# Filling du on TensorE in tiles of 64 rows by 32 columns in place of 64 by 64

## The chip, the cores and the metric

The kernel runs on one core of a Trainium2 chip. The metric is the device time of one execution in microseconds (us), smaller is better. The core has five engines that run side by side and meet through semaphores: TensorE (PE in the rows: matmuls; PEld: the loads of their stationary operand), VectorE (DVE), ScalarE (ACT), GpSimd (POOL) and SyncE (SP, which here only issues DMAs).

## The reference

It is one layer: a Mamba block, then a mixture of experts, each followed by a LayerNorm. The input has 4 sequences of 2048 tokens of width 256. The Mamba block, cut to what matters here:

```python
x_conv = silu(conv(x_in) + conv_b)                 # 512 channels
dt = softplus(dt_low @ dt_proj_w.T + dt_proj_b)    # 512 channels
def step(h, inp):                                  # over time; h is 512 channels x 16 states
    xt, dtt, Bt, Ct = inp
    A_bar = exp(dtt[..., None] * A)
    B_bar = (A_bar - 1.0) / safe_A * Bt[:, None, :]
    h = A_bar * h + B_bar * xt[..., None]
    y = einsum('bds,bs->bd', h, Ct) + D * xt
    return (h, y)
```

The second part routes each token to 2 of 16 experts and adds a shared expert. The change does not touch it.

## The kernel before, in words

The work is cut into 16 units of 512 tokens. A unit has 512 channels (4 chunks of 128 partitions) and 16 states, so 64 items of one chunk and one state. An item passes through three engines: ACT makes exp(dt*A) for it (line 691), DVE runs the recurrence over 512 tokens as one scan (line 1175), POOL multiplies the result with C (line 617), and PE sums the products over the states (lines 930 and 931). `h` and `hc`, which hold the items under way, have 8 slots each.

The scan's additive input is called du. The kernel writes the recurrence so that du at each step is the difference of neighbouring values of B*x, and PE makes these differences: `fill` (lines 952 to 971) multiplies 64 rows of tokens of `x_conv_rows` (the stationary operand, the channels are its columns) with a 64x128 matrix of steps, `b_steps` (the moving operand: 64 token columns for each of two states). The result goes to `g_ps`, which has two buffers of 1024 columns, one for each e. A fill serves one chunk and two states; it consists of 4 blocks of time (k), 2 halves of the rows (r) and, in the innermost loop of line 968, the halves of the 128 channels. There are 32 fills in a unit, 512 in all. Afterwards DVE adds 16 edge values in place (`join`, line 1166) and scans twice from `g_ps` (line 1175). The fill of the next use of the buffer waits for those scans (line 963).

TensorE is addressed in tiles: a matmul of 64 rows and 64 columns takes a quarter of the 128x128 array, and four such matmuls on different quarters can be under way together. The rows of the stationary operand's partitions choose the row half, the partitions of the output the column half. Quarters are used by the fill, by the sums over states (`add_quarters`, lines 926 to 931), by the convolution (line 1036) and by the dt projection (line 1055). The skip product (line 1067) has 17 rows and is placed in tiles of 32 rows by 64 columns. The others (lines 1018, 1021, 1045, 1081, and so on) use the array whole. An fp32 matmul appears in the trace as two records of MATMUL and two of LDWEIGHTS, so the 16 matmuls of a fill are 32 records of each.

The order on PE is written out by hand. For a unit, m runs over the 64 items; tables such as FILL_AT and SUM_AT (lines 334 and 336) say at which m each fill and sum stands, and PLACE (line 328) where the projections, transposes and so on stand between them. Each engine goes through its own order strictly; the counters of the semaphores, du_ready (one step for each fill), scanned, hc_ready and summed, tie them together.

After the last unit comes the second part (from line 1310 on), which does not contain fills.

Of the kernel before, what the change touches and what calls it, by code (L numbers as in the profile page):

```python
# [28 lines left out]
P = 128  # L29
# [37 lines left out]

BY_SCALAR = (2, 4, 6, 7)
HALVES = (slice(0, HALF_ROWS), slice(HALF_ROWS, P))


def count(unit, per, add):

    return per * unit + add
# [12 lines left out]
def wait(eng, sem, value):  # L87

    if value > 0:
        eng.wait_ge(sem, value)  # L90
# [59 lines left out]
def mamba(nc, d):  # L150
# [5 lines left out]
    with ExitStack() as ctx:  # L156
# [241 lines left out]
        def emptied_all(eng, u, tiles):  # L398

            most = {}  # L400
            for t in sorted(tiles, key=ORDER.get):
                most[bank_of(u, t)] = t
            for bank, t in most.items():
                eng.wait_ge(emptied[bank], tiles_before(u, t) + 1)
# [8 lines left out]
        def host(kind, c, u):  # L413

            return u if c >= 2 else u - 1
# [13 lines left out]
        def scalar_steps(j):  # L429
            return sum(k in BY_SCALAR for k in range(j))  # L430
# [479 lines left out]
        def _(pe):  # L910
# [41 lines left out]
            def fill(u, f):  # L952

                q, e = divmod(f, 2)
                j, c = q % HALF, q // HALF * 2 + e
                if q < HALF:
                    if j in BY_SCALAR:
                        pe.wait_ge(steps_by_scalar, count(u, len(BY_SCALAR), scalar_steps(j) + 1))
                    else:
                        pe.wait_ge(steps_by_vector, count(u, JS - len(BY_SCALAR), j - scalar_steps(j) + 1))  # L960
                if j == 0:
                    emptied_all(pe, host("T", c, u), [f"T{c}"])
                wait(pe, scanned, count(u, ITEMS, 4 * (q - 1) + 2 * e + 2))
                for k in range(KB):
                    for r in range(2):
                        rows = slice(HALF_ROWS * r, HALF_ROWS * (r + 1))
                        steps_of = b_steps[rows, j, k].rearrange("p t s -> p (t s)")
                        for some in HALVES:
                            one = nc.tensor.matmul(g_ps[some, e, r * T + k * P:r * T + (k + 1) * P], x_rows[rows, c, k, some],  # L969
                                                   steps_of, start=True, stop=True)  # L970
                one.then_inc(du_ready, 1)

            def tile(u, t, part):
# [72 lines left out]
                elif t in ("d1", "d3"):  # L1046
# [3 lines left out]
                    by_e = ((w_dt, dt_low), (w_dt_again[RANK:], dt_low_again[RANK:]))  # L1050
                    for half, some in enumerate(HALVES):
                        for e, (weights, rows) in enumerate(by_e):
# [6 lines left out]
                elif t in ("r1", "r3"):  # L1059
                    c = int(t[1]) - 1  # L1060
                    if c == 0:
                        pe.wait_ge(both_ready, count(u, 1, 1))
                    for half, some in enumerate(HALVES):
                        for e in range(2):
# [20 lines left out]
            for u in range(-1, UNITS):  # L1085
                if u == 0:
                    pe.wait_ge(routing_made, 7)
                    pe.wait_ge(bias_step, 7)
                    pe.wait_ge(skip_rows_ready, 2)
                for m in range(ITEMS):  # L1090
                    for su, n in due(SUM_AT, m, u):
                        add_states(su, n)
                    if u >= 0 and m in SKIP_ADD_AT:
                        add_skip(u, SKIP_ADD_AT.index(m))
                    for fu, f in due(FILL_AT, m, u):
                        if fu == 0 and f == 0:
                            pe.wait_ge(diags_ready, 2)
                        fill(fu, f)
                    for t, part in parts_at(u, m):
                        tile(u, t, part)  # L1100
                    if u == -1 and m == 7:
                        pe.wait_ge(a_inv_step, 5)
                        for c in range(CH):
                            one = nc.tensor.matmul(y_ps[0:NS, 0, c * P:(c + 1) * P], a_inv[:, c], ident[:], start=True, stop=True)
                        one.then_inc(turned_inv, 1)
# [1105 lines left out]
```

## Time and profile before

| what | value |
|---|---|
| time, median of 2 runs | 2217.26 us (2213.77 to 2220.75) |
| the profiled execution | 2220.81 us |
| its span in the trace | 2218.9 us |
| mean granted TensorE clock | 0.981 of full |
| fills begin and end | 55.5 us and 1844.4 us in the span |
| PE busy | 93% of the span |
| DVE, POOL, ACT busy | 82%, 80%, 78% |

How to read it: the span falls into the units with their fills, up to about 1844 us, and the second part, about 375 us. "Busy" for PE is the time in which at least one matmul record is open. A record lasts until its results are through, so it is longer than the time after which the next may begin; how long the array is taken by something is therefore read from the distance of starts, not from the length of a record.

### The profile page before, as it was taken

The numbers are of one execution on the slowest core, as the hardware profiler recorded it, in microseconds if no ns is written. First come the engines' busy times: TensorE is split into PE (matmuls) and PEld (weight loads), VectorE is DVE, ScalarE is ACT, GpSimd is POOL, SyncE is SP. The second block draws the span as 40 slices with busy tenths as digits, with TensorE's granted clock in tenths as the row PEclk, the third lists the DMA queues.
The fourth block names the chain that finished last, engine by engine and source line by source line (L and its number), as shares of the span: only waits on it lengthen the run. The fifth ranks groups of instructions, "written<-read, shape, count | busy, mean of one in ns | idle before, by whom it ended". The sixth has DMA issues, their size and how long they took to land. (4 is left out here: it accounts for less than half of the span.)

```text
span 2218.9 us, 68067 instructions
## 1 busy us (share of the span) xinstructions
PE 2062.6 (93%) x26118; PEld 1246.7 (56%) x26118; DVE 1825.4 (82%) x3055; ACT 1741.5 (78%) x3561; POOL 1778.1 (80%) x1699
## 2 busy tenths in 40 slices
PE   6899999999999999999999999999999796999996
PEld 2455555555555555555555555555555454788864
DVE  2898899989898989899989898988898994655556
ACT  4888888888888888898989897979898872555537
POOL 2787898979898989898989898988898994566654
PEclk9999999999999999999999999999999999999999
DMA  2232323332333232333232333232323354496668
GB/s 89 68 100 78 109 92 110 92 110 96 111 92 114 88 118 88 110 91 116 88 118 86 113 91 114 90 117 83 114 90 101 103 173 150 139 284 208 194 209 284
DMA packets 152301, 267.42 MB, mean 121 GB/s; under 512 B 26408, under 2 KB 65324, under 8 KB 151470
## 3 DMA queue, kind: packets, MB, share of 16 engines
q1 hardware_dynamic: 137198, 220.93, 33.2%
q0 software_dynamic: 14784, 42.16, 5.4%
q8 instruction: 210, 3.44, 0.6%
q14 instruction: 109, 0.89, 0.1%
HBM read 205.62 MB, written 57.39 MB: 119 GB/s over the span
## 5 line engine op out<-in xcount | busy, mean ns | idle before, releaser
L617 POOL TENSOR_TENSOR hc<-h,c_rep 128x512 f32<-128x512 f32 x1024 | 1286.4, 1278 | 212.5 <-DVE h L1175 164.9
L1175 DVE TENSOR_TENSOR_SCAN h<-g_ps,carry,h 128x512 f32<-128x512 f32 x1024 | 1274.4, 1273 | 71.7 <-ACT h L691 54.1
L691 ACT ACTIVATE h<-dt,a_mat 128x512 f32<-128x512 f32 x1024 | 695.4, 714 | 108.0 <-POOL hc L617 44.6
L969 PEld LDWEIGHTS g_ps<-b_steps,x_conv_rows 64*64 64x64 f32 x16384 | 477.1, 134 | 299.6 <-issue 209.9
L969 PE MATMUL g_ps<-b_steps,x_conv_rows 64*64 64x128 f32 x16384 | 559.0, 274 | 29.8 <-DVE h L1175 24.7
L930 PE MATMUL y_ps<-hc,dg_inv 64*64 64x512 f32 x2048 | 502.8, 605 | 14.8 <-POOL hc L617 6.5
L931 PE MATMUL y_ps<-hc,dg_inv 64*64 64x512 f32 x2048 | 501.4, 605 | 0.0
L930 PEld LDWEIGHTS y_ps<-hc,dg_inv 64*64 64x64 f32 x2048 | 139.5, 135 | 234.1 <-issue 160.4
L1662 POOL DMA_INDIRECT y_planes<-gathered,home x144 | 140.0, 972 | 106.2 <-DVE gathered L2089 81.8
L1855 PE MATMUL banks<-w_up,gathered 128*128 x576 | 148.3, 380 | 2.4 <-ACT gathered L1712 2.4
L1166 DVE TENSOR_TENSOR g_ps<-g_ps,minus_u 128x16 f32<-128x16 f32 x512 | 87.0, 170 | 76.5 <-PE g_ps L969 55.9
L1018 PE MATMUL work<-w_up 128*128 128x512 f32 x256 | 136.4, 659 | 11.5 <-DMA b_in<-in_b_in 7.4
L604 POOL DMA_INDIRECT slot_rows<-x_tok,place x116 | 122.3, 1054 | 26.1 <-issue 17.9
L1036 PE MATMUL work<-room 64*64 64x512 f32 x1024 | 122.7, 592 | 14.4 <-ACT x_conv_rows L766 12.7
L931 PEld LDWEIGHTS y_ps<-hc,dg_inv 64*64 64x64 f32 x2048 | 135.0, 135 | 0.0
L1021 PE MATMUL work<-w_up 128*128 128x512 f32 x256 | 126.0, 611 | 2.2 <-ACT gate L770 1.4
L707 ACT ACTIVATE b_steps<-steps_of,bc_tok 128x64 f32<-128x64 f32 x512 | 127.1, 340 | 0.0
L2072 DVE TENSOR_TENSOR gathered<-gathered,banks 128x128 f32<-128x128 f32 x144 | 41.1, 286 | 96.6 <-ACT gathered L1722 96.2
L1081 PE MATMUL work<-w_out,y_gated 128*128 128x256 f32 x480 | 118.4, 382 | 0.0
L1855 PEld LDWEIGHTS banks<-w_up,gathered 128*128 128x128 f32 x576 | 98.2, 190 | 10.1 <-issue 2.7
L1252 DVE SCALAR_TENSOR_TENSOR x_arg<-work,x_arg 128x512 f32<-128x512 f32 x128 | 85.3, 679 | 21.9 <-ACT work L802 21.3
L1081 PEld LDWEIGHTS work<-w_out,y_gated 128*128 128x128 f32 x480 | 85.6, 191 | 21.1 <-issue 9.8
(277 smaller groups left out, 2879.0 us busy)
## 6 DMA issues: line engine op xcount, KB each, us to landing
c_rep<-bc_rows SPq DMA_DIRECT2D x512, 256.0 KB
gathered<-slot_rows SPq DMA_DIRECT2D x144, 129.5 KB, 2.3
gathered<-y_planes SPq DMA_DIRECT2D x32, 512.0 KB, 8.4
w_up<-in_x_t SPq DMA_DIRECT2D x16, 512.0 KB, 4.8
x_raw<-in_x_tok SPq DMA_DIRECT2D x16, 512.0 KB, 4.9
out<-x_t SPq DMA_DIRECT2D x16, 512.0 KB, 3.1
x_t_rows<-y_gated SPq DMA_DIRECT2D x15, 512.0 KB, 4.3
x_t<-x_t_rows POOLq DMA_DIRECT2D x12, 512.0 KB, 5.4
```

The lines of the kernel that those rows point to most:

```text
L617: nc.gpsimd.tensor_tensor(hc[:, at_all % HCS], h[:, at_all % SLOTS], c_rep[:, at % CS], ALU.mult).then_inc(hc_ready, 1)
L691: nc.scalar.activation(h[:, (ITEMS * u + m) % SLOTS], dt[:, c], ACT.Exp, scale=a_mat[:, c, s:s + 1]).then_inc(factor_ready, 1)
L707: one = nc.scalar.activation(b_steps[:, j, k, :, s % 2], steps[:], ACT.Copy, scale=bc_tok[:, k, s:s + 1])
L930: nc.tensor.matmul(y_ps[first, 0], by[low_rows], v[low_rows], start=start, stop=stop)
L931: return nc.tensor.matmul(y_ps[second, 1], by[high_rows], v[high_rows], start=start, stop=stop)
L969: one = nc.tensor.matmul(g_ps[some, e, r * T + k * P:r * T + (k + 1) * P], x_rows[rows, c, k, some], steps_of, start=True, stop=True)
L1018: mm = nc.tensor.matmul(out, w_in[:, k, m * P:(m + 1) * P], x_t[:, of % 2, k], start=(k == 0), stop=(k == KT - 1))
L1021: mm = nc.tensor.matmul(out, w_in[:, k, m * P:(m + 1) * P], x_t[:, q, k], start=(k == 0), stop=(k == KT - 1))
L1081: mm = nc.tensor.matmul(o, y_gated[:, c, tok:tok + P], w_out[:, c], start=False, stop=(c == CH - 1))
L1175: nc.vector.tensor_tensor_scan(slot, du, slot, carry[:, batch(u), c, s:s + 1], ALU.add, ALU.mult).then_inc(scanned, 1)
L1662: nc.gpsimd.indirect_dma_start(d["y_planes"], bass.IndirectOffsetOnAxis(home[:, k % RING:k % RING + 1], 0), y_slots[:, k % BODY], None).th ...
L1855: one = nc.tensor.matmul(gu_ps[:, k % 2, 0:2 * IF], xt[:, k % 4, h * P:(h + 1) * P], w_up[:, e, h], start=(h == 0), stop=(h == KT - 1))
```

## The change

The innermost loop of `fill` goes over four groups of 32 channels instead of two groups of 64. Each matmul then has 64 rows and 32 columns; eight different tiles (two row halves times four column quarters) take part in the place of four. The moving operand is the same, the output ranges together are the same, one semaphore step still stands at the last matmul. The sums over states and the rest are as before.

```diff
+FOURTHS = tuple(slice(at, at + 32) for at in range(0, P, 32))
...
                     for r in range(2):
                         rows = slice(HALF_ROWS * r, HALF_ROWS * (r + 1))
                         steps_of = b_steps[rows, j, k].rearrange("p t s -> p (t s)")
-                        for some in HALVES:
+                        for some in FOURTHS:
                             one = nc.tensor.matmul(g_ps[some, e, r * T + k * P:r * T + (k + 1) * P], x_rows[rows, c, k, some],
                                                    steps_of, start=True, stop=True)
                 one.then_inc(du_ready, 1)
```

On PE, in the first unit, two fills around the addition of the skip term (the lines below it move down by one; a row's shape is that of the output). Before:

```order
L969 MATMUL g_ps<-b_steps,x_conv_rows 64x128 x16
L930 MATMUL y_ps<-skip,half_ident 64x512
L931 MATMUL y_ps<-skip,half_ident 64x512
L930 MATMUL y_ps<-skip,half_ident 64x512
L931 MATMUL y_ps<-skip,half_ident 64x512
L969 MATMUL g_ps<-b_steps,x_conv_rows 64x128 x16
L930 MATMUL y_ps<-hc,dg_inv 64x512
L931 MATMUL y_ps<-hc,dg_inv 64x512
```

At the same place in the changed kernel:

```order
L970 MATMUL g_ps<-b_steps,x_conv_rows 32x128 x32
L931 MATMUL y_ps<-skip,half_ident 64x512
L932 MATMUL y_ps<-skip,half_ident 64x512
L931 MATMUL y_ps<-skip,half_ident 64x512
L932 MATMUL y_ps<-skip,half_ident 64x512
L970 MATMUL g_ps<-b_steps,x_conv_rows 32x128 x32
L931 MATMUL y_ps<-hc,dg_inv 64x512
L932 MATMUL y_ps<-hc,dg_inv 64x512
```

Nothing changes its place. Each fill has 32 matmuls where it had 16, and where quarters stood beside quarters, tiles of 64 by 32 now stand beside tiles of 64 by 64. Counted over the whole order of PE: the 512 fills form 506 uninterrupted stretches; 332 of them come directly after quarters and 241 have quarters directly behind them. The number of places where the shape of the tile changes from one matmul to the next rises from 586 to 1159, by these 573.

## Rows read from the trace of the kernel before

**Rows 1.** The page: span, busy time, and slices of three engines.
```profile
span 2218.9 us, 68067 instructions
PE 2062.6 (93%) x26118; PEld 1246.7 (56%) x26118; DVE 1825.4 (82%) x3055; ACT 1741.5 (78%) x3561; POOL 1778.1 (80%) x1699
...
PE   6899999999999999999999999999999796999996
...
DVE  2898899989898989899989898988898994655556
...
POOL 2787898979898989898989898988898994566654
```

**Rows 2.** Busy time by stretch: window, length, then each engine, clock, DMA.
```profile
60.00:1844.00 1784.00, 1685.69 (x24225) 965.64 (x24221) 1601.31 (x2244) 1520.54 (x2965) 1550.85 (x1412) 0.98 0.34 103
```

**Rows 3.** Waits, 60 to 1844 us: who, for whom, us in total, times, longest.
```profile
POOL hc L617 <- DVE h L1175: 162.1, 188, 3.4
PEld g_ps L969 <- DVE h L1175: 81.9, 128, 2.8
DVE h L1175 <- ACT h L691: 53.9, 35, 2.2
DVE g_ps L1166 <- PE g_ps L969: 53.0, 96, 3.9
...
ACT h L691 <- POOL hc L617: 44.6, 58, 1.7
ACT gate L770 <- PE work L1021: 44.5, 35, 4.5
...
DVE x_raw L1203 <- PE work L1081: 20.9, 15, 1.5
```

**Rows 4.** Groups of PE by form, 60 to 1844 us: busy, mean ns, idle before.
```profile
L969 PE MATMUL g_ps<-b_steps,x_conv_rows 64*64 64x128 f32 x16303 | 556.3, 274 | 27.6 <-DVE h L1175 24.7 <-ACT x_conv_rows L766 0.7 <-issue 0.4
L930 PE MATMUL y_ps<-hc,dg_inv 64*64 64x512 f32 x2032 | 498.7, 605 | 12.7 <-DVE y_gated L1182 6.0 <-POOL hc L617 4.5
...
L1036 PE MATMUL work<-room 64*64 64x512 f32 x960 | 115.1, 592 | 12.7 <-ACT x_conv_rows L766 12.7
...
L1045 PE MATMUL work<-ident,w_up 128*128 128x128 f32 x248 | 40.4, 286 | 28.7 <-ACT dt L778 22.0 <-ACT w_up L761 2.7 <-ACT room L753 2.4
```

**Rows 5.** Timeline of PE, 1002.3 to 1012.9 us: start us, length us, what.
```profile
1002.74 1.09 PE L1067 MATMUL work<-both,skip_rows 17*64 17x512 f32 x8
1003.76 0.64 PE L930 MATMUL y_ps<-hc,dg_inv 64*64 64x512 f32 x1
...
1004.24 0.59 PE L930 MATMUL y_ps<-hc,dg_inv 64*64 64x512 f32 x1
...
1004.67 0.59 PE L930 MATMUL y_ps<-hc,dg_inv 64*64 64x512 f32 x1
...
1005.10 0.59 PE L930 MATMUL y_ps<-hc,dg_inv 64*64 64x512 f32 x1
...
1005.52 1.05 PE L969 MATMUL g_ps<-b_steps,x_conv_rows 64*64 64x128 f32 x32
1006.51 1.98 PE L1021 MATMUL work<-w_up 128*128 128x512 f32 x4
1008.42 1.10 PE L969 MATMUL g_ps<-b_steps,x_conv_rows 64*64 64x128 f32 x32
1009.35 0.59 PE L930 MATMUL y_ps<-hc,dg_inv 64*64 64x512 f32 x2
...
1011.06 1.05 PE L969 MATMUL g_ps<-b_steps,x_conv_rows 64*64 64x128 f32 x32
1011.94 1.47 PE L1036 MATMUL work<-room 64*64 64x512 f32 x12
```

**Rows 6.** Records of L969 alone at a fill's start: window, length, PE, PEld, clock.
```profile
1001.70:1001.73 0.03, 0.02 (x4) 0.03 (x4) 1.00 0.00 0
1001.73:1001.83 0.10, 0.10 (x4) 0.10 (x8) 1.00 0.00 0
```

**Rows 7.** Groups of the page: weight loads of 64 and of 128 columns.
```profile
L969 PEld LDWEIGHTS g_ps<-b_steps,x_conv_rows 64*64 64x64 f32 x16384 | 477.1, 134 | 299.6 <-issue 209.9
...
L1081 PEld LDWEIGHTS work<-w_out,y_gated 128*128 128x128 f32 x480 | 85.6, 191 | 21.1 <-issue 9.8
```

## The prediction, made before the changed kernel was run

> **What bounds the kernel now.** I read the page's slices first, then the busy time of the stretch with the fills, then the waits, and then the timeline of PE start by start. In the slices PE stands at 9 from the second to the last slice of the units, while DVE and POOL change between 8 and 9 [rows 1]. In numbers, for 60 to 1844 us: PE is busy 1685.7 of 1784.0 us (94.5%), DVE 1601.3, POOL 1550.9, ACT 1520.5 [rows 2]. So PE is the fullest engine and has 98 us of idle time in 16 units; the next has 183 us. It is not the only one that sets the pace. The waits go round: POOL waits for the scans (162 us), PE for the scans before a fill (81.9 us of the weight loads, some of it while matmuls still run), DVE for ACT (53.9 us) and for fills (53.0 us), ACT for POOL (44.6 us), and ACT and DVE for PE's other lines (44.5 us at L1021, 20.9 us at L1081) [rows 3]. PE's own idle time stands at four kinds of places above all: 28.7 us before the transposes of L1045, 27.6 us before fills, 12.7 us each before L930 and L1036 [rows 4]. A microsecond added to PE is therefore neither free nor certain to show in full.
>
> **What one fill costs.** A fill with quarters before and behind takes from 1011.06 to 1011.94, 0.88 us [rows 5]: 16 matmuls of two records on four tiles, so 8 passes of 0.11 us, in each of which four tiles stream 128 columns. A pass over 512 columns takes 0.43 us (1004.67 to 1005.10) [rows 5], four times as long, so the moving columns set the time of a pass. At a start four matmuls and four weight loads fall into 0.03 us; in the next 0.10 us no further matmul starts, only the loads of the next pass [rows 6]. The tiles wait for their streams, not for the issue.
>
> **The change, part by part.**
>
> *The matmuls themselves: 0.* 32 matmuls of two records on eight tiles are again 64/8 = 8 passes. Each streams the same 128 columns, so again 8 x 0.11 = 0.88 us. Twice the tiles do half the width; nothing is won. Four pairs start in 0.03 us, so eight need about 0.05 us of a pass of 0.11 us. The bound below zero is a stream that gets faster in a narrow tile, for which no row speaks; above, it is no overlap beyond four (both are rivals below).
>
> *Weight loads: 0.* Each has 32 columns instead of 64. 134 against 191 ns for 64 and 128 columns [rows 7] makes about 28 ns less for each. In the middle of a fill they lie under the previous pass. At a fill's first pass they are exposed, which would save at most 506 x 0.03 = 15 us; against that, the last of eight tiles starts about 0.03 us later than the last of four, at 506 exits. I let them cancel.
>
> *Changes of the tile's shape: the price.* The rows show what it costs to change the shape on PE. A fill that is followed by a matmul of another shape takes from 1005.52 to 1006.51, 0.99 us, 0.11 more than the 0.88 above. A fill that comes after another shape and has quarters behind it takes from 1008.42 to 1009.35, 0.93 us: its first pass is 0.05 us longer, because the load of the second can no longer hide. The skip product L1067 (32-row tiles) between a fill and L930 shows both: 1002.74 to 1003.76 is 1.02 us for two passes of 0.43, 0.16 more; and the first pass of L930 behind it takes 0.48 us (1003.76 to 1004.24) instead of 0.43 [rows 5]. So a change of shape costs 0.11 + 0.05 = 0.16 us on PE. The change makes 573 new ones: 332 into a fill, 241 out of one. 573 x 0.16 = 92 us. The bounds: 0 if only another row height or the whole array makes PE stop (the nearest row, L1067, changes the height and not the width), and 573 x 0.16 + 15 = 107 us with the later last tile and no gain at the loads. I take 92, because L1021 and L1067 differ from quarters in different ways and cost the same. The Trainium skill, "TensorEngine Tiling (Array Packing)", Key Properties, says that changing the tiling mode, though not changing the tile, drains TensorE, and it lists 64x64 and 64x32 as different modes. By that rule the lower bound of 0 goes away and the 92 us stand; the trace agrees as far as it shows changes (0.16 us each), but it has none of width alone between row halves.
>
> *What of the 92 us reaches the end.* All of it lies in the stretch up to 1844 us; the second part has no fill. If all of PE's 98 us of idle time [rows 2] took up the new work, nothing would show; if none did, 92 us would. The idle time is at waits for the scans, for dt, for hc and for x_conv [rows 4], and the engines behind those wait in turn for PE [rows 3]: fills that come later make later scans, so part of such a wait moves along instead of shrinking. Against that, of DVE's 183 us of idle time only 53.0 + 20.9 are ended by PE, so much of the ring runs without PE setting it. I take two fifths (39 us) as absorbed and three fifths of the idle time as staying: 92 - 39 = 53 us. What is late next is the join after each fill, then the scan, then POOL's multiplication.
>
> *Instructions.* PE gets 32768 more of them, on 68067 [rows 1]. I cost this at 0: the fetch runs beside the work, and four pairs in 0.03 us show that dispatch keeps up.
>
> The sum: 2220.8 us of the profiled execution + 53 = 2274 us. That execution lies 3.5 us above the median of the runs, so against the median it is 2217 + 53 = **2270 us**, 2.4% slower. 2% of this kernel is 44 us, about what a measurement can tell from no change.
>
> **The rivals.**
>
> *It is absorbed, or a change of width alone is cheap.* If PE stays in step when only the width changes, or the ring takes up more than half of the 92 us, the time lies between 2217 and 2261. For it: 98 us of idle time, and waits of PE for DVE at 128 loads of fills, where a stop of 0.11 us would be hidden. Against: PE at 94.5% would have to reach 97 to 99.6% of the old stretch. Chance 0.32.
>
> *The eight do not all run at once.* In the whole trace the closest sustained matmuls are the 32 records of a fill in 0.88 us, 27 ns apart. If that is a floor of issue, of the weight path or of the reading of the moving operand, which would now feed four column tiles from the same rows, 64 records take 1.76 us. That adds 0.88 x 512 = 451 us, with the 92 us 543, less at most 98 us of idle time: 2217 + 445 to 543, about 2700 us. Any smaller stretch counts too: 10 ns on each of 4096 passes are 41 us. For it: such short intervals between eight tiles are not in the trace. Against: within a pass four pairs start in 0.03 us [rows 6]. Chance 0.13, a third of it for a moderate stretch up to about 2400. The Trainium skill, "TensorE: Matmul & The Clock Gate", says in the section "Wait — 56ns, not 53.3ns?" that starts never come closer than about 25 ns. By that rule a fill would take 64 x 25 ns = 1.6 us and the kernel, by an estimate from that page, about 2217 + 0.72 x 512 + 92 - 50 = 2630 us. Here the trace disagrees inside a pass: four starts lie in 0.03 us.
>
> *Faster: a narrow tile streams faster.* If the 0.11 us of a pass belonged not to the 128 moving columns but to the 64 stationary columns (a load and its use per tile), half the width would shorten it. From 0.09 us a pass on, the shape changes are paid back (8 x 512 x 0.0225 = 92 us); at 0.055 us a fill takes 0.44 us, PE loses 225 us and gains 92, and DVE with 183 us of idle time becomes the bound: about 2217 - 80 = 2137 us. Against it: passes of 512 columns with the same 64 stationary columns take 0.43 us, four times as long [rows 5]. Chance 0.04.
>
> **How the numbers follow.** Forecast 0.51, absorbed 0.32, stretched 0.13, faster 0.04. The forecast's own range is from 2248 to 2300 (40 to 90% of 92 us). It and the absorbed case meet at 2261, the line of 2%, and a little of the forecast lies below it: faster 0.04, same 0.34, slower 0.62. For the range I leave out below the faster case and nearly complete absorption (0.10 together) and above the strong stretch (0.09): 2232 to 2350 us.
>
> **What would show it.** Right: 32768 records of the fill line with mean near 274 ns; a fill from first to last start in about 0.8 us; 1.04 us (0.88 + 0.16) from a fill's start to the matmul behind it where it stands between quarters; PE busy time up by about 90 us before the last fill; weight loads near 106 ns. Absorbed: the same rows, but PE's idle time falls by over 45 us. Cheap width: quarters follow a fill with no extra 0.11 us. Stretched: fills above 0.95 us between first record and next line, PE near 99%. My number is wrong above all if the share that reaches the end is not 0.6, which no row gives directly.

## The result and the profile after

The changed kernel takes 2286.24 us (median of 2 runs, 2283.78 to 2288.7) against 2217.26 us before: ratio 1.0307 [1.0289, 1.0325], 69 us slower. The forecast was 2270 us (+53), in a range of 2232 to 2350. The profiled execution took 2283.78 us, 63.0 more than the profiled one before.

The page of the changed kernel (compare [rows 1]; the last row is the queue that brings instructions: packets, MB, share):

```profile
span 2281.8 us, 100835 instructions
PE 2172.5 (95%) x42502; PEld 1233.5 (54%) x42502; DVE 1818.6 (80%) x3055; ACT 1744.9 (76%) x3561; POOL 1780.5 (78%) x1699
...
PE   6899999999999999999999999999999897999997
...
DVE  2898888888888879888988888988888985555557
...
q8 instruction: 338, 5.54, 1.0%
```

PE's busy time rose by 110 us; DVE, ACT and POOL do the same work in the same time. The row of the q8 queue was 210 packets before. 128 packets more for 32768 instructions more: a packet holds 256 instructions.

The busy time by stretch, from 60 us to the end of the last fill, which is now at 1907.9 us (1844.7 before, compare [rows 2]):

```profile
60.00:1907.90 1847.90, 1795.49 (x40566) 951.97 (x40562) 1595.17 (x2244) 1523.84 (x2964) 1553.61 (x1413) 0.98 0.33 101
```

This stretch is 63.2 us longer, which is the whole difference; the second part takes 374 us in both. In the stretch PE's busy time rose by 109 us (1686.4 to 1795.5) and its idle time fell from 98.3 to 52.4 us. The granted clock is 0.98 as before.

The waits in this stretch (who, for whom, us in total, times, longest; compare [rows 3]):

```profile
POOL hc L618 <- DVE h L1176: 187.5, 203, 3.7
DVE g_ps L1167 <- PE g_ps L970: 115.6, 159, 3.0
PEld g_ps L970 <- DVE h L1176: 60.8, 74, 1.6
...
ACT gate L771 <- PE work L1022: 47.1, 42, 4.8
...
DVE h L1176 <- ACT h L692: 40.0, 33, 1.5
```

DVE now waits for fills 115.6 us instead of 53.0, and PE's loads for the scans 60.8 instead of 81.9. So PE came after DVE more often than before, and POOL's wait for the scans grew with it (162 to 187.5).

The groups of PE in the same stretch (busy, mean ns, idle before with its releasers; compare [rows 4]), and after them the page's group of the fill's loads (compare [rows 7]):

```profile
L970 PE MATMUL g_ps<-b_steps,x_conv_rows 64*32 64x128 f32 x32640 | 609.5, 276 | 23.1 <-DVE h L1176 11.0 <-issue 10.3 <-ACT x_conv_rows L767 0.6
L931 PE MATMUL y_ps<-hc,dg_inv 64*64 64x512 f32 x2034 | 505.5, 613 | 1.4 <-DVE y_gated L1183 1.4
...
L1037 PE MATMUL work<-room 64*64 64x512 f32 x960 | 117.1, 601 | 11.6 <-ACT x_conv_rows L767 11.6
...
L1046 PE MATMUL work<-ident,w_up 128*128 128x128 f32 x248 | 40.3, 286 | 10.1 <-ACT dt L779 7.1 <-DVE x_arg L1253 1.3
```

```profile
L970 PEld LDWEIGHTS g_ps<-b_steps,x_conv_rows 64*32 64x32 f32 x32768 | 465.1, 106 | 375.2 <-issue 310.1
```

The idle time went down above all before the transposes (28.7 to 10.1 us), before the sums (12.7 to 1.4) and, for scans, before fills (24.7 to 11.0). What is new is 10.3 us before L970 ended by "issue": PE stood still with nothing to wait for in any other engine. The loads take 106 ns (134 before), as forecast.

The timeline around two fills (start, length, what; compare [rows 5]):

```profile
1005.15 0.64 PE L931 MATMUL y_ps<-hc,dg_inv 64*64 64x512 f32 x1
1005.16 0.64 PE L932 MATMUL y_ps<-hc,dg_inv 64*64 64x512 f32 x1
1005.19 0.64 PE L931 MATMUL y_ps<-hc,dg_inv 64*64 64x512 f32 x1
1005.21 0.64 PE L932 MATMUL y_ps<-hc,dg_inv 64*64 64x512 f32 x1
...
1008.74 1.16 PE L970 MATMUL g_ps<-b_steps,x_conv_rows 64*32 64x128 f32 x64
1009.83 0.64 PE L931 MATMUL y_ps<-hc,dg_inv 64*64 64x512 f32 x1
...
1010.31 0.59 PE L931 MATMUL y_ps<-hc,dg_inv 64*64 64x512 f32 x1
...
1010.74 0.59 PE L931 MATMUL y_ps<-hc,dg_inv 64*64 64x512 f32 x1
...
1011.70 1.33 PE L970 MATMUL g_ps<-b_steps,x_conv_rows 64*32 64x128 f32 x64
1012.97 0.28 PE L1080 MATMUL work<-b_out_parts,full 65*128 65x256 bf16 x1
```

A fill between other shapes takes 1.09 us (1008.74 to 1009.83), where 1.04 was forecast; from its first start to its last it is 0.89 us in the median (0.81 before). The first pass of quarters behind it takes 0.48 us, the second 0.43: the exposed load of 0.05 us is there. The next fill takes 1.27 us. And the four quarters at 1005.15 start over 0.06 us; in a pass where the instructions are queued they start within 0.03 us [rows 6].

A stop inside a fill, in the timeline of PE, and the packets of the instruction queue from 1058.0 to 1058.5 us:

```profile
1058.04 1.12 PE L970 MATMUL g_ps<-b_steps,x_conv_rows 64*32 64x128 f32 x61
1060.36 0.41 PE L970 MATMUL g_ps<-b_steps,x_conv_rows 64*32 64x128 f32 x3 [1.20 <-issue]
1060.69 1.10 PE L1003 MATMUL work<-w_up,w_x 128*96 128x512 f32 x2
```

```profile
q8 instruction: 1, 0.02, 11.7%
```

61 of 64 records run, then PE is idle for 1.20 us and the last three follow. 2.2 us before it goes on, the transfer of a packet of 16384 bytes of instructions begins. I call such a gap a fetch stop: over 250 ns between two starts inside one fill, no other engine that ends it, and such a packet begun 2.0 to 2.8 us ahead of the resume. There is none in the trace before, and there are 17 after (14.4 us by the distance of starts, 9.9 us of it with PE idle), which resume 2.2 to 2.7 us after their packet begins. Gaps at a fill's first record that end with a scan are not counted, though a packet precedes some of them too; they are waits for DVE.

### The profile page after: what moved, and what is told of

It is laid out like the page before. It is cut to its first block and busy times, and to the rows that moved or that the text cites. A ratio compares the mean times of both kernels' runs of the same rounds, so it can differ in the third digit from the quotient of the medians.

```text
span 2281.8 us, 100835 instructions
## 1 busy us (share of the span) xinstructions
PE 2172.5 (95%) x42502; PEld 1233.5 (54%) x42502; DVE 1818.6 (80%) x3055; ACT 1744.9 (76%) x3561; POOL 1780.5 (78%) x1699
## 5 line engine op out<-in xcount | busy, mean ns | idle before, releaser
L970 PEld LDWEIGHTS g_ps<-b_steps,x_conv_rows 64*32 64x32 f32 x32768 | 465.1, 106 | 375.2 <-issue 310.1
L970 PE MATMUL g_ps<-b_steps,x_conv_rows 64*32 64x128 f32 x32768 | 611.8, 276 | 25.2 <-DVE h L1176 11.0
L931 PE MATMUL y_ps<-hc,dg_inv 64*64 64x512 f32 x2048 | 509.0, 613 | 3.0 <-POOL hc L618 1.4
L932 PE MATMUL y_ps<-hc,dg_inv 64*64 64x512 f32 x2048 | 508.8, 613 | 0.0
L931 PEld LDWEIGHTS y_ps<-hc,dg_inv 64*64 64x64 f32 x2048 | 133.7, 135 | 246.1 <-issue 207.2
L605 POOL DMA_INDIRECT slot_rows<-x_tok,place x116 | 122.1, 1053 | 25.8 <-issue 17.6
L932 PEld LDWEIGHTS y_ps<-hc,dg_inv 64*64 64x64 f32 x2048 | 132.6, 135 | 0.2
L1856 PEld LDWEIGHTS banks<-w_up,gathered 128*128 128x128 f32 x576 | 98.2, 190 | 10.1 <-issue 2.7
L1082 PEld LDWEIGHTS work<-w_out,y_gated 128*128 128x128 f32 x480 | 85.6, 191 | 21.5 <-issue 10.1
L803 ACT ACTIVATE work<-square,shifts 128x512 f32<-128x512 f32 x128 | 85.5, 682 | 13.4 <-DVE x_arg L1253 11.4
```

The lines of the kernel that those rows point to most:

```text
L931: nc.tensor.matmul(y_ps[first, 0], by[low_rows], v[low_rows], start=start, stop=stop)
L932: return nc.tensor.matmul(y_ps[second, 1], by[high_rows], v[high_rows], start=start, stop=stop)
L1082: mm = nc.tensor.matmul(o, y_gated[:, c, tok:tok + P], w_out[:, c], start=False, stop=(c == CH - 1))
L1856: one = nc.tensor.matmul(gu_ps[:, k % 2, 0:2 * IF], xt[:, k % 4, h * P:(h + 1) * P], w_up[:, e, h], start=(h == 0), stop=(h == KT - 1))
```

## The experiments

Two causes could add up to the 69 us: the 573 new changes of shape, and 16384 more matmul records with as many loads, which must be supplied. The first four runs set the one against the other (Theory A: shape alone; the rival B: instructions alone). When each failed in its pure form, the following were judged by a mixed Theory C: about 0.06 us of the end for a new change and 4.6 ns for an additional matmul. Every ratio is against runs of the kernel before on the same chip. Each of the three groups ran on a chip of its own (before: 2216.38, 2244.41 and 2250.01 us); the second part took 374 us on the first and 395 to 404 us in the runs on the others, so only ratios are compared between groups. The last column has the mean granted clock of the kernel's runs and of those of the kernel before beside them (for the change, of the two profiled executions).

| run | shape changes | PE records | ratio to before | clock: run, before |
|---|---|---|---|---|
| before | 586 | 26118 | 1 | |
| the change | 1159 | 42502 | 1.0307 [1.0289, 1.0325] | 0.981, 0.981 |
| e1_all_narrow | 586 | 48134 | 1.0411 [1.0381, 1.0441] | 0.970, 0.981 |
| e2_sums_narrow | 1067 | 30470 | 1.0205 [1.0188, 1.0222] | 0.970, 0.981 |
| e3_short_moving | 586 | 42502 | 1.0165 [1.0148, 1.0182] | 0.972, 0.981 |
| e4_half_narrow | 1436 | 34310 | 1.0301 [1.0282, 1.0319] | 0.976, 0.981 |
| f1_row_halves | 1159 | 17926 | 1.0252 [1.0218, 1.0286] | 0.974, 0.980 |
| g_before | 449 | 26118 | 1.0291 [1.0254, 1.0329] | 0.966, 0.980 |
| g_after | 465 | 26118 | 1.0922 [1.0888, 1.0956] | 0.955, 0.980 |
| i_changed (the change) | 1159 | 42502 | 1.0420 [1.0392, 1.0449] | 0.974, 0.976 |
| i_row_halves (f1) | 1159 | 17926 | 1.0217 [1.0190, 1.0245] | 0.974, 0.976 |
| i_one_of_two | 847 | 34310 | 1.0085 [1.0057, 1.0113] | 0.974, 0.976 |
| h_skip64 | 522 | 26118 | 0.9975 [0.9955, 0.9995] | 0.975, 0.976 |

The clock is a third thing that can differ. At its lower level (1.2 GHz, 0.5 in the rows) a fill takes 1.57 us from its first start to its last in the trace before (median of four), at the upper level (2.4 GHz) 0.81. In the stretch of fills PE was at the lower level for 58 us before, 65 us with the change and 99 us in each of e1, e2 and e3. Among 94 executions, each compared with the mean of its own kernel, a granted clock lower by 0.01 went with a time longer by 13 us. By that figure the clock would be about 15 us of the loss of e1 and e2, 12 of e3 and 7 of e4 and f1 each. This is an estimate; no run holds the clock fixed, and the lower clock may itself come from what the kernel does. The change itself hardly differs from before in it.

**More instructions and no new change of shape.** The first run is the changed kernel with the sums split as well (the diff shows the first of the two sums), and the second sum, the convolution and the dt projection likewise:

```diff
-                nc.tensor.matmul(y_ps[first, 0], by[low_rows], v[low_rows], start=start, stop=stop)
+                for half in range(2):
+                    to, of = slice(first.start + 32 * half, first.start + 32 * half + 32), slice(32 * half, 32 * half + 32)
+                    nc.tensor.matmul(y_ps[to, 0], by[low_rows, of], v[low_rows], start=start, stop=stop)
...
```

> The changed kernel, with the other work that stood in quarters (sums over states, skip addition, convolution, dt projection) in tiles of 64 by 32 as well. Fills have as many matmuls as in the changed kernel, PE even more in all (24589 against 21773 and 13581 before), but the shape of the tile changes as often as before the change (586 times, not 1159). Theory A (the time went into the new changes of shape, 0.16 us each on PE, and about 0.05 us at the late end of a fill): no new change is left, the late end counts only at the 265 fills not followed by this shape; PE gets some 10 us, the time is 2217 to 2232 us. Rival B (the doubled instructions of the fills cost it, shape or not): 2286 us or more.

2304.34 us, slower than the change itself. Theory A expected nearly the time of before and failed. The waits of PE, 60 us to the last fill:

```profile
PE g_ps L975 <- issue: 44.2, 52, 3.1
PE g_ps L975 <- DVE h L1183: 12.3, 15, 3.3
```

44.2 us of PE's idle time stand before fill records without another engine to wait for; after the change alone it is 10.3 us. Fetch stops counted as above: 53, 57.5 us.

The third splits the moving columns instead of the stationary ones, so it has the instructions of the change and no new shape:

```diff
+                    for at in (0, HALF_ROWS):
+                        for r in range(2):
...
+                            for some in HALVES:
+                                to = r * T + k * P + at
+                                one = nc.tensor.matmul(g_ps[some, e, to:to + HALF_ROWS], x_rows[rows, c, k, some],
+                                                       steps_of[:, at:at + HALF_ROWS], start=True, stop=True)
```

> The kernel before, its fills in quarters, but each matmul split into two of 64 moving columns: as many matmuls in a fill (32) as in the changed kernel, no new change of shape. In the changed kernel starts come every 16.7 ns from about the 43rd record of a fill on, so with 64 records some 42 at the pace of the array (0.57 us) and 22 at 16.7 ns (0.37 us): 0.94 us in place of 0.88 for a fill. Theory A: +0.06 x 512 = 31 us on PE, 2225 to 2245 us. Rival B: as the changed kernel, 2286 us.

2254.11 us, +1.65%: above A's range and below B's figure. PE's waits in its stretch of fills:

```profile
PE g_ps L971 <- issue: 19.5, 23, 1.8
```

There are 27 fetch stops, 25.8 us. So a kernel with the change's number of instructions and no new shape loses about half of what the change loses. Not all of it is supply: four quarters with 64 moving columns follow the last four after 0.059 us, more than half of the 0.109 us for 128 columns, which adds about 37 us on PE over 512 fills (estimate), and the clock was lower (above).

**New changes of shape, few new instructions.** The second run is the kernel before with nothing changed but `add_quarters`, whose two sums are split as in the first run's diff:

> The kernel before, its fills in quarters; only the sums over states and the skip addition are in tiles of 64 by 32. 1067 changes of shape against 586 before, so 481 new ones, with 2176 more matmuls where the changed kernel has 8192 more. Theory A: 481 x 0.16 = 77 us on PE, of which about 0.6 shows: 2255 to 2280 us. Rival B (instructions): a quarter of the 69 us at most, below 2236 us.

2261.37 us, +45 us for 481 new changes: A held, B failed. There is not one fetch stop in a fill. This is the run in which shapes of the change (64 by 32 beside 64 by 64) cost time with few new instructions. Its PE is busy 1766.9 us of its stretch, 80.5 us more than before:

```profile
60.00:1885.20 1825.20, 1766.90 (x28600) 930.58 (x28603) 1604.08 (x2248) 1521.91 (x2970) 1556.38 (x1415) 0.97 0.34 101
```

The fourth puts a change inside each fill:

```diff
-                        for some in FOURTHS:
+                        for some in (FOURTHS if k < KB // 2 else HALVES):
```

> The changed kernel, but in each fill only the first two blocks of time are in tiles of 64 by 32, the last two in quarters: half of the additional matmuls (4096), but 1436 changes of shape, 850 more than before and 277 more than the changed kernel. Theory A: 850 x 0.16 = 136 us on PE, slower than the changed kernel, 2295 to 2320 us. Rival B: half of the loss, about 2252 us.

2284.06 us, between the two theories: +68 us for 850 new changes, 0.080 us each, with only 38.0 us of PE idle time left in the stretch (98.3 before).

The counterpart, with fewer instructions than before, fills in tiles of 64 rows by all 128 columns, two at once:

```diff
-                        for some in HALVES:
-                            one = nc.tensor.matmul(g_ps[some, e, r * T + k * P:r * T + (k + 1) * P], x_rows[rows, c, k, some],
-                                                   steps_of, start=True, stop=True)
+                        one = nc.tensor.matmul(g_ps[:, e, r * T + k * P:r * T + (k + 1) * P], x_rows[rows, c, k],
+                                               steps_of, start=True, stop=True)
```

> The kernel before, with the fills in tiles of 64 rows by 128 columns, two at once: 8 matmuls in a fill in place of 16 (before) or 32 (changed), the same 8 passes of 128 columns, and the same 1159 changes of shape as the changed kernel. Theory A (changes of shape alone make the loss of 69 us): about 2286 us, if anything more, as the first load has 128 columns. Theory C (both: about 0.06 us of end time for a new change of shape, about 4.6 ns for an additional matmul through the supply of instructions): 573 x 0.06 = 34 us, and some 10 us for the longer first loads: 2240 to 2268 us. Theory B (supply alone): at most 2217 us.

2297.38 us, +2.52% or 53 us, above C's figure (up to 51 us) and below A's (69). It has the same 573 new changes of shape as the change and 8192 records fewer than before, has no fetch stop, and is still slower. So something other than the supply of instructions costs over 2%. But it is not the changes of shape alone. The timeline around a fill of f1, and its stretch of fills:

```profile
1001.28 1.16 PE L968 MATMUL g_ps<-b_steps,x_conv_rows 64*128 64x128 f32 x16
1002.38 0.64 PE L930 MATMUL y_ps<-hc,dg_inv 64*64 64x512 f32 x1
```

```profile
60.00:1896.50 1836.50, 1792.42 (x16102) 992.72 (x16103) 1602.13 (x2247) 1523.90 (x2970) 1551.03 (x1414) 0.98 0.33 100
```

Its fill takes 1.10 us between other shapes, as long as the narrow one (1.09), and PE is busy 106 us more than before, against 109 with the change. Its first loads have 128 columns: the second pass starts 0.213 us after the first, where later ones follow after 0.112. So 0.10 us a fill is its own first load; the narrow fill loses 0.024 us there and 0.08 us at its last pass (below).

**Fewer changes of shape by order.** If a change costs 0.16 us of PE, moving fills next to work of another shape should pay:

In g_before the other work of every fourth item stands ahead of its fill:

```diff
+                    if m % 4 == 2:
+                        for t, part in parts_at(u, m):
+                            tile(u, t, part)
...
-                    for t, part in parts_at(u, m):
+                    for t, part in parts_at(u, m) if m % 4 != 2 else ():
```

> The kernel before, fills in quarters; where m modulo 4 is 2 the parts of the other tiles go to PE before the fill, not behind it, so that the fill stands directly ahead of the sums more often. 449 changes of shape against 586, as many matmuls. Theory C: 137 fewer changes at 0.06 us: 8 us faster, 2205 to 2212 us, unless the fills, which come later by one or two matmuls of 0.85 us, make the scans wait. Theory B: no change from the changes of shape.

In g_after it stands behind the next sums and fill:

```diff
-                    for t, part in parts_at(u, m):
-                        tile(u, t, part)
+                    for at in {2: (), 3: (m - 1, m)}.get(m % 4, (m,)):
+                        for t, part in parts_at(u, at):
+                            tile(u, t, part)
```

> The kernel before; the parts that stand where m modulo 4 is 2 go to PE one item later, behind the sums and the next fill. 465 changes of shape against 586, as many matmuls; fills come no later, projections and transposes up to 2.6 us later. Theory C: 121 x 0.06 = 7 us faster, 2205 to 2214 us, unless ACT, which takes those tiles, becomes late. Theory B: 2217 us.

Both missed: +2.9% and +9.2%. The waits of g_before and then those of g_after, each over its own stretch of fills:

```profile
DVE g_ps L1169 <- PE g_ps L969: 166.0, 111, 4.9
```

```profile
POOL hc L617 <- DVE h L1176: 381.4, 209, 7.1
...
ACT score L727 <- PE work L993: 80.9, 15, 7.1
```

In g_before each moved fill comes late and DVE waits 166.0 us for fills instead of 53.0. In g_after other products come late and ACT with them, and POOL's wait for the scans rises from 162 to 381.4 us. PE's idle time went from 98.3 to 159.6 and 257.6 us, for 137 and 121 saved changes, worth 22 and 19 us of PE. The clock fell as well: in g_after PE was at the lower level for 221 us of the stretch (58 before), and its busy time is 60 us longer with not one matmul more. In these runs the order on PE was worth more than the shapes, with the clock's part not separated.

**The disputed cost by itself.** In the next, blocks with the shape and number of a fill's matmuls run alone on PE ahead of the first unit, on data that is there (their results are not used): 40 in quarters, 40 in narrow tiles, 20 pairs in alternation, 40 in quarters with 64 moving columns.

```diff
+            def alone_narrow():
+                for k in range(KB):
+                    for r in range(2):
+                        rows = slice(HALF_ROWS * r, HALF_ROWS * (r + 1))
+                        for quarter in range(4):
+                            some = slice(32 * quarter, 32 * quarter + 32)
+                            nc.tensor.matmul(y_ps[some, r, k * P:(k + 1) * P], w_in[rows, 0, some], w_in[rows, 1, k * P:(k + 1) * P], start=True, stop=True)
...
+            for _ in range(40):
+                alone_narrow()
```

> The kernel before, and ahead of its first unit 160 blocks of matmuls on PE alone whose results are not used: 40 in the form of a fill in quarters, 40 in tiles of 64 by 32, 20 pairs of one and the other in turn, and 40 in quarters with 64 moving columns. No waits between them. 128 columns on four tiles: 0.874 us each in every theory. Theory A: narrow blocks also 0.874, a pair 2 x 0.874 + 2 x 0.16 = 2.07 us. Theory C: narrow blocks and short ones are held at 16.7 ns for each pair of load and matmul, 1.07 us a block, with stops of up to 2 us where instructions have to be fetched; a pair about 2.1 us, as the stops let the supply catch up. Theory B: narrow blocks 1.07 us or more, a pair 0.874 + 1.07 us.

Its windows: the quarters, the narrow blocks, the short ones (length, PE busy, loads busy, other engines, clock):

```profile
7.40:45.10 37.70, 37.46 (x1280) 36.77 (x1280) 11.18 (x35) 1.54 (x2) 0.00 (x0) 1.00 0.13 38
45.20:117.80 72.60, 44.69 (x2563) 39.26 (x2560) 0.00 (x0) 0.00 (x0) 0.00 (x0) 0.93 0.02 4
171.40:243.70 72.30, 41.90 (x2568) 39.21 (x2560) 0.00 (x0) 0.00 (x0) 0.00 (x0) 1.00 0.02 5
```

40 blocks take 37.7 us in quarters, 0.94 a block (the first two take over 1.7 each, over twenty behind them 0.874), and 72.6 us in narrow tiles, 1.81 a block. A narrow block in which no stop falls takes 0.874 too. The short ones, which have the same number of instructions and no narrow tile, take the same 1.81. Every theory had expected far less. The timeline of PE from 60 to 68 us shows where it goes, and below it are the packets of the instruction queue from 60.1 to 60.3 us and from 45.3 to 117.8 us:

```profile
62.80 2.02 PE L1099 MATMUL y_ps<-w_up 64*32 64x128 f32 x128 [1.72 <-issue]
66.26 2.00 PE L1099 MATMUL y_ps<-w_up 64*32 64x128 f32 x127 [1.45 <-issue]
```

```profile
q8 instruction: 1, 0.02, 39.7%
...
q8 instruction: 19, 0.31, 1.8%
```

128 records, with their 128 loads one packet of 256 instructions, run in about 2 us; then PE stands still until the next packet is in, 2.6 us after its transfer began. 19 packets, 19 stops. The supply gives 256 instructions per 3.6 us (72.6 us for 20 times 256), 14 ns for each. Quarters alone use 256 in 4 x 0.874 = 3.50 us, which is just about that rate: after over twenty blocks without a stop they have some as well, the longest with 0.50 us between two starts. Narrow tiles would use them up in half the time.

The alternating part, from 117.8 to 122 us:

```profile
117.83 1.10 PE L1091 MATMUL y_ps<-w_up 64*64 64x128 f32 x32
118.87 1.14 PE L1099 MATMUL y_ps<-w_up 64*32 64x128 f32 x63
120.66 0.27 PE L1099 MATMUL y_ps<-w_up 64*32 64x128 f32 x1 [0.66 <-issue]
120.86 1.10 PE L1091 MATMUL y_ps<-w_up 64*64 64x128 f32 x32
```

A block of quarters between narrow ones takes 1.04 us (117.83 to 118.87; 1.034 by the records) where it takes 0.874 among its own kind: 0.16 us more, 0.05 at its first load and 0.11 before the next block may start. There is one change of shape for each block, and nothing differs in it but the width of the tile. 15 of the 20 blocks of quarters take this 1.034; the others have a stop. The narrow block takes 1.087 where no stop falls in it, 0.21 us more than among its own kind: 0.11 before the next block may start, 0.024 at its first load and the rest at its last pass. That is as long as a fill of the changed kernel.

**The change again beside its parts.** Four kernels on a third chip. First the change as it is, and the row halves of f1:

> The changed kernel again, to stand beside the next ones on one chip. Ratio to the kernel before as at first, 1.029 to 1.0325.

> The fills in tiles of 64 rows by 128 columns again (8 matmuls a fill, 1159 changes of shape), beside the changed kernel on one chip. Theory A (changes of shape alone): the same ratio as the changed kernel or above. Theory C (both): a ratio of about 1.025 beside 1.031, so that some 50 to 55 us belong to the changes of shape and some 15 us to the supply of instructions, as the trace of the changed kernel has 15.4 us of stops within fills that end 2.2 to 2.7 us after an instruction transfer starts.

2342.93 us, +4.2%, outside the expected 2.9 to 3.3%; the row halves repeated their 2.2 to 2.5% with 2300.22 us. So the row halves cost 50 us on this chip, their own first loads included, and the narrow tiles, with 24576 records more, a further 43 us. PE's waits in the stretch of i_changed:

```profile
PE g_ps L970 <- issue: 24.2, 65, 1.2
```

24.2 us in 65 waits, against 10.3 in 14 on the first chip. By the records there are 74 gaps over 250 ns inside fills that no other engine ends, 44.4 us in all: 19 are fetch stops as before (15.2 us), 55 (29.2 us) are mostly about 0.6 us long and come at repeating places in the program. Their cause is open, and so is why this chip shows them. But their sum fits: the change is 43 us behind the row halves here, beside 44 us of stops; on the first chip it lost 69 us where the row halves lost 53 on the second, a difference of 16 us beside 14 us of stops. The expectation for the row halves had 15.4 us of stops for the first chip; that was the idle time of 19 gaps, two of which are waits for scans.

Narrow tiles for one of the two g_ps buffers:

```diff
-                        for some in FOURTHS:
+                        for some in (HALVES if e else FOURTHS):
```

> The changed kernel with tiles of 64 by 32 only in the fills of even chunks (e = 0), the others in quarters: 847 changes of shape, 261 new ones in place of 573, and 4096 additional matmuls in place of 8192. Theory C: 261/573 of the 53 us and, as fills in quarters between let the supply catch up, less than half of the 15 us: 24 + 5 = 29 us, a ratio of about 1.013. Theory B (supply alone): half of the loss, 1.015.

2271.22 us, +0.85%, lower than both theories: 21 us in the medians for 261 new changes and 8192 more records, with no fetch stop. So half of the additional instructions, with a fill in quarters between, brought none of the stops.

Last, a change of shape taken away from the kernel before. The skip product's rows are padded from 17 to 33 with zeros that POOL writes once at the start, which places it in quarters like its neighbours:

```diff
-                            rows = slice(e * HALF_ROWS, e * HALF_ROWS + NS + 1)
+                            rows = slice(e * HALF_ROWS, e * HALF_ROWS + 33)
```

> The kernel before, with the rows of the skip product (L1067) filled up with zeros from 17 to 33, so that it goes to quarters in place of tiles of 32 by 64. 522 changes of shape in place of 586, no more matmuls, the same array time. Theory C: 64 x 0.16 = 10 us less on PE, about half of it at the end: 3 to 6 us faster, a ratio of 0.997 to 0.9985, better than both kernels. If changes of shape cost nothing here: 1.000.

2246.29 us against 2250.01: ratio 0.9975 [0.9955, 0.9995], as expected. By the ratio 64 changes fewer gave 5.6 us (1 to 10 by the interval), 0.088 us each. It is the only kernel of the study below before, and by far less than 2%.

## Why the prediction was right, and where it was not

**What bounds the kernel: right.** PE at 94.5% with a ring of waits around it. Its added work showed in part.

**The matmuls themselves, 0: right for the passes.** In the middle of a fill eight starts come per 0.109 us, so eight tiles do run at once, and a narrow block alone takes the same 0.874 us as one of quarters. That removed the stretched rival. The Trainium skill, "TensorE: Matmul & The Clock Gate", section "Wait — 56ns, not 53.3ns?", gives a floor of about 25 ns between starts. The traces disagree for matmuls on different tiles: 7 ns apart within a pass, 16 to 17 ns late in a narrow fill.

**Changes of shape, 573 x 0.16 = 92 us of PE: right, a little high.** Before a fill the last start of the sums stands 519 ns ahead instead of 409, behind it the sums start 199 ns after the fill's last record instead of 89: 110 ns each way. The exposed load is 0.05 us at the quarters behind a fill and 0.024 at the narrow first pass, so 0.16 is a little high for the entries: 332 x 0.134 + 241 x 0.16 = 83 us. m1_alone gives the same 0.16 at a block of quarters for width alone, and e2 gives 45 us at the end for 481 changes, lower clock included. This also settles the absorbed rival's "width is cheap". That f1 and i_row_halves lose 50 to 53 us, the forecast's own number, is a coincidence and no confirmation of the term: their PE time has the first loads of 128 columns in it. The rule of the Trainium skill, "TensorEngine Tiling (Array Packing)", Key Properties, cited in the prediction (a change of mode drains, 64x64 and 64x32 being different modes) holds here, with 0.11 us for the drain.

**Weight loads and the later last tile, "they cancel": wrong.** The loads behaved (106 ns), and their gain at a first pass is 0.027 us. The last of eight tiles was taken to start 0.03 us later than the last of four; that holds in a fill's first pass (0.047 us after the first tile against 0.020). Counted over all fills, the starts of the last pass spread over 99 ns instead of 20. Over the first 37 or so records of a fill the starts of a pass come 7 ns apart, after that mostly 16 to 17 ns apart. A pass still begins every 0.109 us, so this costs nothing until the last pass, where it shows in full: 0.079 x 512 = 40 us of PE against 12 to 14 us gained.

**Instructions, 0: the step that failed.** The argument was that four pairs in 0.03 us show that dispatch keeps up. They show how close four starts can lie, not how fast instructions arrive. m1_alone measured the arrival: 256 instructions per 3.6 us. The kernel before has no stop from it; the changed one uses up more than arrives for the length of each fill, and the quarters between fills, 16 records in 1.9 us, use less. Where that does not make up for it, PE stops: 17 times, 14.4 us. That the wider spacing late in a fill (above) comes from the supply as well would fit, but was not shown.

**What reaches the end, three fifths: partly luck.** By starts, PE's added work comes to about 138 us: 63 us from the first to the last start of fills (later last pass and stops included), 63 us before and behind them (573 x 0.11) and 12 us at the loads of quarters behind fills. That is 92 less 9 at the entries and 5 at entries that changed shape before too, plus 40 for the last pass and 20 for the stops (14) and what is left. By busy time it comes to 109 us. Idle time took 46 us (39 forecast), and 63 us (69 in the medians) reached the end. That is 0.58 of 109, as the prediction's 53 is of 92; but the 92 was worked out from starts, and of 138 it is only 0.46. So the sum was too small by 46 us and the share too large, and the two errors partly cancelled. How the 69 us divide was not measured apart. The row halves added about 118 us of PE by starts and lost 50 to 53; at that rate the change's own shapes, some 80 us, are about 35 us of the end, the later last pass most of the next 18, and the stops the last 16 (estimates). Theory C's 0.06 us for a change, fitted to the first runs, gives 34. On the third chip, where the stops were 44 us, the same forecast was 40 us too low: the number was good partly because this chip was. One slip in the range: 40% of 92 us above 2217 is 2254, not 2248.

**The rivals.** Absorbed: failed, although its sign, idle time down by over 45 us, came true (46), since more was added than it had assumed. Faster: failed, no pass got shorter. Stretched: failed in its size, since passes kept their 0.109 us; of its mild form only the last pass of a fill remains.

## What to carry to other kernels

Before splitting a matmul into more tiles, ask whether the number of moving columns falls. If not, nothing is gained, and there are two prices: 0.16 us for each place where a block of one tile shape meets the other shape, width included, and the instructions. Look at the rate of instructions over a packet's worth (256 in about 3.6 us here), not at how closely four starts stand. And before taking another kernel with the same shape changes as the measure of their cost, compare the length of one block in both: here 1.09 and 1.10 us had different causes. An order on PE that brings other engines' inputs in time was worth more here than grouping equal shapes.

## What the runs showed of the hardware that was not expected

- PE's instructions come in packets of 16384 bytes, 256 instructions. Where PE went on using them faster than one in about 3.6 us, it stopped until the next was in, 2.2 to 2.7 us after its transfer began in the changed kernel. With PE working alone, blocks with twice the instructions took 1.81 us against 0.94.
- A change between tiles of 64x64 and 64x32 costs the same as one between whole array and quarters: 110 ns for PE to run empty, and the first load, which nothing hides: 24, 50 and 101 ns for 32, 64 and 128 columns.
- The change costs 3.1% on one chip and 4.2% on another, while the row halves cost 2.5% and 2.2% on two. The narrow tiles, with the most instructions, differ most. What makes the 55 short stops on the third chip was not tried and stays open.
